# First attention of a fused transformer: the three pieces of a group's values in one run, behind the unit's maxima products

## What is computed

```
scores   = einsum('bhqd,bhkd->bhqk', q, k) / SCALE
out_std  = einsum('bhqk,bhkd->bhqd', softmax(scores, -1), v)
scores_p = einsum('bhqd,bhkd->bhqk', q, kp) / SCALE
out_p    = einsum('bhqk,bhkd->bhqd', softmax(scores_p, -1), v)
out = alpha * out_std + (1.0 - alpha) * out_p
h   = h + out.transpose(0, 2, 1, 3).reshape(B, T, C) @ W_O.T
```

## Time and profile before

| | |
|---|---|
| median of 3 runs | 1941.53 us (1939.67 to 1943.0) |
| the profiled execution, its own time | 1939.7 us |
| its span, first to last instruction | 1937.9 us |
| mean granted TensorE clock over the span | 0.974 |
| TensorE busy | 1780.5 us, 92% of the span |
| VectorE busy | 1008.1 us, 52% |
| ScalarE busy | 674.1 us, 35% |

### The profile page before, as it was taken

The page is one execution under the profiler, slowest core; times in us unless marked ns, Lnnn a source line. Parts: engine busy times, 40 slices in busy tenths (PEclk is TensorE's granted clock), DMA queues, the critical chain, the costliest instruction groups (busy, mean ns, idle before and its releaser), DMA issues. The chain is left out here.

```text
span 1937.9 us, 29556 instructions
## 1 busy us (share of the span) xinstructions
PE 1780.5 (92%) x10095; PEld 1156.9 (60%) x10095; DVE 1008.1 (52%) x2080; ACT 674.1 (35%) x1287; POOL 409.3 (21%) x417
## 2 busy tenths in 40 slices
PE   6798999989999996899957999998999999999997
PEld 4454344444444433577743566666667667999997
DVE  4586778768777875788845544452321111222221
ACT  2104656556565674455522322332211110111110
POOL 1300210211201000798821221111032120101010
PEclk9899999999999997999988999999999999999999
DMA  5943436435444212000029100000010002242211
GB/s 135 167 66 38 75 63 87 75 40 96 73 57 78 36 58 86 1 0 0 0 69 342 35 0 0 0 1 1 1 41 25 24 33 93 102 164 101 98 35 32
DMA packets 112564, 117.53 MB, mean 61 GB/s; under 512 B 11470, under 2 KB 104400, under 8 KB 112209
## 3 DMA queue, kind: packets, MB, share of 16 engines
q1 hardware_dynamic: 99312, 87.93, 22.0%
q10 hardware_dynamic: 9504, 18.88, 2.7%
q0 software_dynamic: 3648, 9.46, 1.3%
HBM read 80.87 MB, written 35.29 MB: 60 GB/s over the span
## 5 line engine op out<-in xcount | busy, mean ns | idle before, releaser
L795 DVE TENSOR_REDUCE mx<-ps_a 128x1 f32<-128x384 f32 x768 | 384.5, 551 | 87.0 <-PE ps_a L501 84.9
L699 ACT ACTIVATE prob<-ps_a 128x768 f32<-128x768 f32 (+1 forms) x512 | 306.2, 650 | 116.6 <-PE ps_a L514 116.5
L501 PE MATMUL ps_a<-ks,qs 96*128 96x384 bf16 x768 | 214.6, 334 | 19.4 <-DMA ks<-parts_dram 9.9
L514 PE MATMUL ps_a<-qs,ks 100*128 100x384 bf16 x768 | 207.6, 330 | 10.3 <-issue 5.1
L1966 PEld LDWEIGHTS ps_e<-xTr,w 128*128 128x128 f32 x1792 | 206.0, 193 | 2.2 <-issue 0.8
L1966 PE MATMUL ps_e<-xTr,w 128*128 128x128 f32 x1792 | 206.3, 276 | 0.6 <-DVE xTr L2139 0.6
L1902 PE MATMUL ps_e<-xT_all,w 128*128 (+1 forms) x512 | 169.8, 491 | 0.9 <-ACT xT_all L1993 0.9
L501 PEld LDWEIGHTS ps_a<-ks,qs 96*128 96x128 bf16 x768 | 61.5, 98 | 172.8 <-DVE mx L795 101.6
L525 PE MATMUL ps_a<-prob,vp 128*32 128x384 f32 x1536 | 163.3, 498 | 0.0
L1902 PEld LDWEIGHTS ps_e<-xT_all,w 128*128 128x128 f32 x512 | 97.5, 192 | 66.5 <-issue 1.8
L2029 ACT ACTIVATE gel_r<-ps_e 128x512 f32<-128x512 f32 x56 | 33.4, 597 | 281.1 <-PE ps_e L1966 281.1
(11 more groups left out here) (241 smaller groups left out, 2642.5 us busy)
## 6 DMA issues: line engine op xcount, KB each, us to landing
ks<-parts_dram SPq DMA_DIRECT2D x192, 96.0 KB, 6.7
w<-in_L_ffn_W_dram ACTq DMA_DIRECT2D x18, 1024.0 KB, 7.6
parts_dram<-parts SPq DMA_DIRECT2D x24, 576.0 KB, 3.7
qs<-parts_dram SPq DMA_DIRECT2D x96, 96.0 KB, 4.2
prob<-in_x_dram SPq DMA_DIRECT2D x24, 256.0 KB, 5.8
w<-in_L_ffn_W_dram SPq DMA_DIRECT2D x6, 1024.0 KB, 12.1
grouped_x<-empty_row SPq DMA_DIRECT2D x1, 4352.0 KB, 24.2
grouped_h<-empty_row SPq DMA_DIRECT2D x1, 4240.5 KB, 35.0
```

Source lines behind the costliest of these rows:

```text
L501: mm = pe.matmul(ps[:, r % 3, 0:T], qs[0:NS, b, u // 2, t * P:(t + 1) * P], ks[0:NS, b, u % 2, u // 2], start=True, stop=True)
L514: mm = pe.matmul(ps[:, 4 + t, 0:T], ks[0:NS + 4, b, kp, hh, t * P:(t + 1) * P], qs[0:NS + 4, b, hh], start=True, stop=True)
L699: act.activation(prob[:, g % 2, j, ts.start:ts.stop], ps[:, 4 + ts.start:4 + ts.stop, 0:T], ACT.Exp).then_inc(exp_done.sem, 1)
L795: dve.tensor_reduce(at, ps[:, r % 3, 0:T], AX.X, ALU.max).then_inc(ring_free.sem, 1)
```

## The change

In a unit with j = 1, all three pieces of the values of the group before are now written, one behind the other, and behind both maxima products that end the unit; units 2 and 3 of a group have none. Every matmul is the same as before, and so are all instructions of the other engines.

```diff
@@ -572,12 +572,13 @@
                         if more:
                             ring(i + 1, 1 - b, ring_part(v)[:1])
                         scores(i, b, v, 1)
-                        if j and g:
-                            values(i, b, g - 1, j - 1)
-                        elif j and prev:
-                            values(i - 1, 1 - b, GROUPS - 1, j - 1)
                         if more:
                             ring(i + 1, 1 - b, ring_part(v)[1:])
+                        for t in range(TT):
+                            if j == 1 and g:
+                                values(i, b, g - 1, t)
+                            elif j == 1 and prev:
+                                values(i - 1, 1 - b, GROUPS - 1, t)
                         step, n, of = bank3(v, prev, more, more2)
                         if step:
                             last = in_bank3(step, i + of, n, last)
```

## The result

The changed kernel takes 1971.47 us (median of 4 runs, 1970.58 to 1976.04) against 1941.78 before: ratio 1.0159, 95% interval 1.0141 to 1.0177. It is slower by 30 us. The forecast was slower by 20, 1961, in a range of 1946 to 1976.

What follows compares the result with a forecast made beforehand. The prediction took TensorE, 92% busy, to be only a little ahead of VectorE. Its terms, 11.8 + 1.6 + 1.9 + 5.2 = 20.5 us on 1939.7, gave 1960, stated as 1961 for the median; range 1946 to 1976.

Steps and rivals of the forecast that it cites:

- the floor of the relieved units: Units without a piece and bank-3 step can't go below 1.40 us, so each gives back 0.47, not 0.88.
- Why VectorE is emptied: Around each run VectorE gets some 3 us without a new product and idles about 1.5 us per group.
- The ledger of the fifth image: Unit-by-unit sum of how much later each group of the fifth image ends, reaching +2.4 us at group 7.
- the 0.41 of the sum: Wait for bank 3 behind a project step in a unit without a piece: 2.69 us against 2.28, 0.41.
- five middle images: Five images like the fifth, each 2.36 us later: 11.8 us.
- the first 1.6: First image, with no run before unit 5 and no output steps: +1.6 us.
- the seventh 1.9: Seventh image, without project steps, only light groups and one with moments: +1.9 us.
- the last 5.2: Last image: runs delay turn_outputs and output 0, for which VectorE's quantizing waits; 5.2 us late at the end.
- The rival in which it falls in the last image: Granted clock falls in the last image, up to 2 us in each of eight groups: 1965 to 1975; chance 8%.
- the forecast case: The unit-by-unit sum of delays over all images holds: 1950 to 1972 us; chance 62%.
- The faster rival: TensorE is the bound and saves 0.47 us in each of 63 groups: 1912, or some 1927; chance 8%.
- the slower rival: VectorE becomes the bound, each run leaving it idle with no unit making that up: 1975 to 1985; chance 12%.

## Why the prediction held, and where it was short

**The direction and the mechanism were right.** TensorE's own work fell as computed: 2.14 us per run, next instruction 2.07 behind its start. What takes it back is the floor of the relieved units at 1.40 (measured 1.40 and 1.44), and that floor is shown, not only argued: halving both engines' work moved it to 1.08 and turned the sign of the change. Of the 29.7 us, 12 go when VectorE's reductions are halved (29.7 - 17.7), and these are waits for VectorE in the units of runs, the transpose and the new moments. Another 22 (17.7 + 4.3) go when the exponentials are halved on top. That halving the reductions alone left units 26 and 27 at 1.40 and 1.44 shows that the turn-round of scores and exponentials is enough to hold them. It doesn't show that VectorE's floor isn't: behind the run its nine reductions take 4.29 us, 1.43 for each three, so it stands at the same height. No kernel with halved exponentials and whole reductions was run, so how the 22 us divide between the two floors stays open. The starved VectorE that I described in "Why VectorE is emptied" starves for 1.11 us instead of 1.5, and its idle time in front of the reductions rose by 10 us to 96.9, where I had expected 120.

**The ledger of the fifth image**, forecast and measured, how much later each group ends: 0.1 and 0.2; -0.15 and 0.3; -0.1 and 0.2; 0.5 and 1.0; 0.95 and 1.65; 1.9 and 2.7; 2.45 and 3.3; 2.4 and 3.2. The single units are close: unit 1 +1.73 (forecast 1.72), unit 14 -0.43 (-0.47), unit 15 -0.25 (-0.26), unit 23 +0.02 (0), unit 30 -0.47 (-0.47). The image is short by 0.8 us, and half of it is one term. A bank-3 step directly behind a run takes 0.1 us longer (1.40 for 1.29), in units 5, 13, 17 and 21: 0.4 us that my sum had at nothing. A step that starts after a wait, as in units 14, 18 and 19, takes 0.1 longer too, but it comes only 0.35 late and not the 0.41 of the sum, so 0.04 is missing in each. Unit 7 stays at 1.80, where ScalarE has two copies and I had let it have one; unit 8 then costs less, so this mostly moved. The rest is 0.04 to 0.07 each in the first group and in units 9, 11, 25 and 27.

**By part**: five middle images 11.8 forecast, 18.0 measured; the first 1.6 and 2.7; the seventh 1.9 and 3.9; the last 5.2 and 7.2. The sum is 20.5 and 31.7. The term that was mis-sized is that of an image: 2.36 us in the sum, 3.2 to 3.5 measured where the clock did not fall. (By its own figures the prediction should also have said 1962 and not 1961: 20.5 on 1939.7, and 1.8 for the median.)

**The clock.** The rival in which it falls in the last image, at 8%, came true in part, besides the forecast case. The 1971.5 lie inside its 1965 to 1975 as well, but they didn't get there by its sum: it gave up to 2 us to each of eight runs of the last image, and one fall there cost 1.5. The falls at the start of other images were in no term. In the trace after, the granted clock falls to 1.2 GHz for 3.4 us at the start of the second, sixth and seventh image and twice in the last; before, at none of these places. At the start of the seventh, TensorE was busy 1.42 us of the 3.00 before the fall, with the transpose and the maxima of the next image waited for; unit 0 takes 3.23 us there, and 1.98 in the kernel with the step first, whose clock didn't fall there. In the last image a run falls into such a stretch:

```profile
744.68 0.89 PE L514 MATMUL ps_a<-qs,ks 100*128 100x384 bf16 x3
...
745.50 3.55 PE L525 MATMUL ps_a<-prob,vp 128*32 128x384 f32 x24
...
748.98 0.66 PE L514 MATMUL ps_a<-qs,ks 100*128 100x384 bf16 x3
```

It takes 3.48 us to the next scores instead of 2.07. Unit 17 is 1.5 us longer than its like, and it lies ahead of output 0, where VectorE waits. Together the falls are some 2.8 us in the seven images (an estimate from units 0 and 1: 0.4 in the second, 0.9 in the sixth, 1.5 in the seventh) and 1.5 in the last, over a third of the 11 by which I was short. Spreading the last image again removed both falls there.

**What didn't come.** The faster rival: with whole reductions and exponentials the relieved units never went below 1.2. Some 23 us of the pieces' busy time did go (163.3 to 140.6), but TensorE spent them waiting. The Trainium skill, in TensorEngine Tiling (Array Packing), Key Properties, says that a change of the tiling mode drains TensorE. The trace agrees, with 0.88 us for a lone piece against 0.645 inside a run. That pieces are float32 and their neighbours bf16 is not the reason, as the "values" steps show: they are float32 of 128 columns between the same neighbours, and one of eight records takes 1.73 us, one of four 0.87, with nothing left over for the change of type. The rule says nothing about who waits. The Trainium skill's rule on rotating banks (Perfetto Trace Analysis, Matmuls) was behind the slower rival; no run here changed the number of banks, and the 12 of 30 us that went with the halved reductions are no measure of it.

## What to carry to other kernels

A small matmul group that costs a drain may still be worth more spread out, if each unit has a floor set by another engine's turn-round: the piece then fills time that TensorE would wait anyway. Before gathering work, take the relieved unit's floor from a place in the trace where that work is missing already (here the last image, whose units show 1.40), and subtract only what lies above it. And ask of each place what wait the moved work covered there: the waits for bank 3 in units 14 and 18 and for VectorE in unit 23 had been hidden behind a piece, and those for bank 3 in units 13 and 17 turned out to be hidden behind the run, when a step was put in front of it.

## What the runs showed of the hardware

- A step of float32 matmuls of 128 columns takes 0.1 us longer when it stands directly behind those of 32 columns than directly behind bf16 matmuls: a project step 1.40 us until the next scores instead of 1.29, the second step of "values" 0.97 instead of 0.87. A project step behind bf16 matmuls that had to wait, as in unit 14, where TensorE idled 0.19 us before it, takes 1.39 too.
- The granted clock fell for 3.4 us at the start of the second, sixth and seventh image of the change, with TensorE busy 1.67, 1.87 and 1.42 of the 3 us before, and such a fall cost 0.4 to 1.5 us. It did not fall at the start of the sixth image before the change, with the same 1.87 of 3 us busy there: these rows don't tell when it falls.
- The turn-round of scores and exponentials is 1.40 us with exponentials of 768 and 384 columns, whose pair is recorded with 1.19, and 1.08 with half of the columns, whose pair takes 0.71: it fell by 0.32 where the work fell by 0.48.
